# Closing pass of an adaLN block with attention and a mixture of experts: the residual add goes from GpSimd to VectorE, and half of the pair sums go from VectorE to TensorE

## The reference

```python
h = _layernorm(x, axis=-1) * (1 + ca) + sa
x = x + ga * _L0_attn_ref(h, ...)
h = _layernorm(x, axis=-1) * (1 + cb) + sb
x = x + gb * _L0_ffn_ref(h, ...)      # inside: return h + alpha * moe_out
```

## Time and profile before

| | us |
|---|---|
| three timed runs | 453.78, 459.27, 459.58 |
| their median | 459.27 |
| the profiled execution | 455.82 |
| its span (first to last instruction in the trace) | 454.0 |
| TensorE busy | 365.8 (81%) |
| VectorE busy | 312.9 (69%) |
| ScalarE busy | 268.6 (59%) |
| GpSimd busy | 258.4 (57%) |
| closing pass, from the first load's issue to the end of the span | 425.39 to 454.0 |

### The profile page before, as it was taken

One profiled execution on the slowest core, in us unless ns is written; L12 is line 12 of the kernel. 1 busy time (PEld: TensorE's weight loads), 2 busy tenths in 40 slices (PEclk: granted clock), 3 DMA queues, 4 the chain that ended last, 5 costly groups with the idle time before them and its releaser, 6 DMA issues.

```text
span 454.0 us, 11788 instructions
## 1 busy us (share of the span) xinstructions
PE 365.8 (81%) x3935; PEld 300.1 (66%) x3935; DVE 312.9 (69%) x948; ACT 268.6 (59%) x468; POOL 258.4 (57%) x306
## 2 busy tenths in 40 slices
PE   3728889988999999998779998939999999999100
PEld 1415667765766766665447997939999999998000
DVE  2506899999899999999967765624544444444194
ACT  2326789986888888886556668423555555554000
POOL 3010255878789898888763684654444444444264
PEclk9967999997999999999868999887999999999755
DMA  8355666656666666666865122231222122121494
GB/s 274 82 135 142 163 161 158 157 148 169 155 169 179 163 180 180 174 164 168 291 241 141 48 70 60 61 94 43 60 65 66 53 55 58 51 55 43 118 299 138
DMA packets 56027, 59.37 MB, mean 131 GB/s; under 512 B 7167, under 2 KB 48128, under 8 KB 55712
## 3 DMA queue, kind: packets, MB, share of 16 engines
q1 hardware_dynamic: 51648, 50.15, 42.4%
q0 software_dynamic: 4320, 8.47, 5.6%
HBM read 34.81 MB, written 24.23 MB: 130 GB/s over the span
## 4 chain that ended last, share of the span: by engine, by line
PE 35%; POOL 20%; SPq 14%; DMA 12%; issue 10%; DVE 5%; ACT 1%; POOLq 0%; ACTq 0%; DVEq 0%
PE SC L643 19%; POOL queue L1398 10%; PE OB L655 9%; DMA qdram<-rope 4%; POOL rstd L1390 3%; POOL gbh L1379 3%; SPq L352 3%; SPq L332 2%; SPq L362 2%; DVE pt L1313 2%; SPq L386 2%; DMA ydram<-ysb,xb 2%; PE FA L557 2%; SPq L347 2%; DMA stq<-qdram 2%
## 5 line engine op out<-in xcount | busy, mean ns | idle before, releaser
L1435 POOL DMA_INDIRECT ydram<-ysb,xb x71 | 69.4, 977 | 84.2 <-DVE ysb L1223 74.2
L643 PE MATMUL SC<-xTs,wgu 128*128 128x128 f32 x852 | 110.6, 281 | 4.6 <-issue 3.6
L643 PEld LDWEIGHTS SC<-xTs,wgu 128*128 128x128 f32 x852 | 103.1, 196 | 7.4 <-issue 5.8
L711 ACT ACTIVATE pt<-SC 128x1536 f32<-128x1536 f32 x64 | 92.6, 1447 | 25.9 <-PE SC L471 25.8
L944 DVE SCALAR_TENSOR_TENSOR pt<-pt,cst 128x1024 f32<-128x1024 f32 x64 | 81.2, 1268 | 13.6 <-ACT pt L711 13.5
L1398 POOL DMA_INDIRECT queue<-pl,dest x64 | 74.3, 1161 | 15.4 <-issue 14.8
L471 PE MATMUL SC<-stq,stk 24*128 24x256 f32 (+1 forms) x1024 | 64.1, 367 | 15.9 <-DMA stq<-qdram 12.0
L780 ACT ACTIVATE sg<-SC 128x384 f32<-128x384 f32 x71 | 34.8, 490 | 70.0 <-PE SC L643 69.4
L1157 DVE COPY xTs<-FA 128x128 f32<-128x128 f32 x71 | 20.7, 291 | 73.1 <-PE FA L557 64.6
L471 PEld LDWEIGHTS SC<-stq,stk 24*128 24x128 f32 x1024 | 49.3, 197 | 31.3 <-DMA stq<-qdram 13.5
L772 ACT ACTIVATE wgu<-gu,ws 128x704 f32 x71 | 62.1, 875 | 12.2 <-issue 12.1
(11 more groups left out here) (156 smaller groups left out, 524.4 us busy)
## 6 DMA issues: line engine op xcount, KB each, us to landing
stk<-kdram SPq DMA_DIRECT2D x64, 96.0 KB
stq<-qdram SPq DMA_DIRECT2D x64, 96.0 KB
xb<-queue SPq DMA_DIRECT2D x71, 65.0 KB, 1.8
kdram<-rope SPq DMA_DIRECT2D x32, 128.0 KB
qdram<-rope SPq DMA_DIRECT2D x32, 128.0 KB
bc<-modrow SPq DMA_DIRECT2D x16, 256.0 KB
pt<-ydram SPq DMA_DIRECT2D x16, 256.0 KB, 5.2
gu<-gup SPq DMA_DIRECT2D x1, 2816.0 KB
```

The costliest lines, as they stand in the source:

```text
L643: last = mm(GUB[b % 2][:, n, c * P:(c + 1) * P], wgu[:, b % 2, n, c * P:(c + 1) * P], xTs[:, b % DEEP, :], start=True, stop=True)
L711: af(pt[:, j, :, 0:S + P], SC[:, :, 0:S + P], ACT.Exp, scale=SCALE).then_inc(s["exp_done"], 1)
L1435: G.indirect_dma_start(ydram, bass.IndirectOffsetOnAxis(xb[:, slot(b), D + 1:D + 2].bitcast(u32), 0), ysb[:, slot(b), :], None, bounds_che ...
```

## The change

GpSimd's loop of 8 residual adds is gone, with its wait for `base_ready`. VectorE has the residual add now, as a third step of each chunk, and waits for `base_ready` once. The product with the gate is written to `ybuf[1]` and not in place. In chunks 1, 3, 5 and 7 VectorE no longer adds y0 and y1. TensorE does: it multiplies each with the identity matrix and lets the two products accumulate in a bank of PSUM, and VectorE's gate product reads that bank. Each of the four chunks has a bank of its own (FA, FB, BK, OB); the new semaphore `sum0` counts the finished banks.

```diff
+        SUMS = {1: FA, 3: FB, 5: BK, 7: OB}
 ...
+            need(pe, s["y_ready"], NBLK)
+            for n, bank in SUMS.items():
+                pe.wait_ge(s[f"yin{n}"], 2 * DMA)
+                for k in range(2):
+                    last = mm(bank[:, :], ident, ybuf[k][:, n * TCH * D:(n + 1) * TCH * D],
+                              start=(k == 0), stop=(k == 1))
+                last.then_inc(s["sum0"], 1)
 ...
             dve.wait_ge(s["gba_in"], DMA)
+            dve.wait_ge(s["base_ready"], B)
             bch = TCH // T
             for n in range(NCH):
-                dve.wait_ge(s[f"yin{n}"], 2 * DMA)
                 c0, c1 = n * TCH * D, (n + 1) * TCH * D
-                tt(ybuf[0][:, c0:c1], ybuf[0][:, c0:c1], ybuf[1][:, c0:c1], ALU.add).then_inc(s["sum1"], 1)
-                dve.wait_ge(s["sum1"], n + 1)
+                if n in SUMS:
+                    dve.wait_ge(s["sum0"], n // 2 + 1)
+                    both = SUMS[n][:, :]
+                else:
+                    dve.wait_ge(s[f"yin{n}"], 2 * DMA)
+                    tt(ybuf[0][:, c0:c1], ybuf[0][:, c0:c1], ybuf[1][:, c0:c1], ALU.add).then_inc(s["sum1"], 1)
+                    dve.wait_ge(s["sum1"], n // 2 + 1)
+                    both = ybuf[0][:, c0:c1]
                 for m in range(bch):
-                    y = ybuf[0][:, c0 + m * T * D:c0 + (m + 1) * T * D].rearrange("p (t d) -> p t d", d=D)
-                    last = tt(y, y, gba[:, n * bch + m:n * bch + m + 1, :].to_broadcast([P, T, D]), ALU.mult)
+                    part = slice(m * T * D, (m + 1) * T * D)
+                    last = tt(ybuf[1][:, c0:c1][:, part].rearrange("p (t d) -> p t d", d=D),
+                              both[:, part].rearrange("p (t d) -> p t d", d=D),
+                              gba[:, n * bch + m:n * bch + m + 1, :].to_broadcast([P, T, D]), ALU.mult)
                 last.then_inc(s["sum2"], 1)
+                dve.wait_ge(s["sum2"], n + 1)
+                tt(xall[:, c0:c1], xall[:, c0:c1], ybuf[1][:, c0:c1], ALU.add).then_inc(s["sum3"], 1)
 ...
-            pool.wait_ge(s["base_ready"], B)
-            for n in range(NCH):
-                pool.wait_ge(s["sum2"], n + 1)
-                c0, c1 = n * TCH * D, (n + 1) * TCH * D
-                G.tensor_tensor(xall[:, c0:c1], xall[:, c0:c1], ybuf[0][:, c0:c1], ALU.add).then_inc(s["sum3"], 1)
```

More of the change, by code:

```diff
@@ L271, in adaln_kernel @@
         GUB, XP, YP = (SC[:, 0:2, :], SC[:, 2:4, :]), FA, OB
+        SUMS = {1: FA, 3: FB, 5: BK, 7: OB}
         names2 = """table_step table_ready pad_ready padded z_wgu wgu_ready gba_in xt_done xts_ready gu_done
             sg_ready hid_ready y_done y_ready yin0 yin1 yin2 yin3 yin4 yin5 yin6 yin7
-            sum1 sum2 sum3 out_done""".split()
+            sum0 sum1 sum2 sum3 out_done""".split()
         s.update({n: sem(n) for n in names2})
```

## The result

| | before | changed |
|---|---|---|
| median of 17 runs each, us | 458.89 | 454.18 |
| lowest and highest | 453.78, 465.19 | 451.36, 457.39 |
| profiled execution | 455.82 | 453.18 |
| its span | 454.0 | 451.4 |
| issue of the first load | 425.39 | 426.43 |

The ratio of the times, changed over before, is 0.9928, with a 95% interval from 0.9901 to 0.9955. Of 458.89 us that is -3.3 us (-4.5 to -2.1). Times and profiles are compared between undisturbed executions; only the profile of e5 is of one that was 2.3% above the fastest of its kernel, and e6 was run just once.

The account below looks back on a forecast made before the run. VectorE, slowed by GpSimd, was taken to bound the closing pass, and GpSimd's drain the end. VectorE's 1.4 us and the drain's 2.4 made -3.8 us; from a 457.5 us median that gave 453.7, range 449.0 to 458.6.

Parts of the forecast that it names:

- VectorE slowed by GpSimd: Closing pass: without GpSimd's additions product pairs take 0.76 us, not 1.70; last residual add 1.4 us earlier.
- Products from PSUM cost the same: VectorE's gate products reading a PSUM bank: no difference taken from SBUF; some 65 ns more each by the skill.
- TensorE's first sum: Chunk 1 on TensorE at half clock: about 3.6 us, making VectorE wait 3.9 us once.
- The later sums: Chunks 3, 5, 7 on TensorE at half clock: ready at 438.9, 442.4, 446.0, no further wait of weight.
- The rival of a sum at 4.5 us: TensorE's weight loads stand between matmuls: 4.8 us a sum, time 458.5, deciding from 4.5 us; chance 0.03.
- The drain: GpSimd's closing drain at the program's end moves under the closing pass, over by 432; 2.4 us of SyncE's wait go.
- The sum: Whole kernel: span from 454.0 to 450.2 us, a change of -3.8 us; time named 453.7 us.

Follow-up runs that it names:

- e5: Changed kernel plus ten unread TensorE matmuls before the first sum, and the last chunk's residual add and store in two halves; ratio to before 0.9862.
- e6: Changed kernel, but TensorE forms each of its four sums twice into the same bank; one run, 454.29 us beside a before median of 457.59.
- e3: Changed kernel plus one GpSimd memset of 128x2 that waits for the last residual add and that nobody reads; ratio to before 1.0012.
- e1: Changed kernel without TensorE's sums: VectorE adds y0 and y1 in all chunks, GpSimd stays out of the pass; ratio to before 0.9928.
- e2: Changed kernel plus ten unread fp32 TensorE matmuls of 512 columns between the last block and the first sum; ratio to before 0.9862.
- e9: Second run of the changed kernel plus ten unread TensorE matmuls before the first sum; ratio to before 0.9868.

## Why the prediction was right, point by point

**VectorE slowed by GpSimd: right.** The products take 0.76 us a pair everywhere, and an even chunk 438.00 to 440.12 = 2.12 us (2.15 predicted). The last residual add came 1.4 us earlier in the pass, as forecast.

**Products from PSUM cost the same: right.** The rows by their source:

```profile
L1329 DVE TENSOR_TENSOR pt<-pt,stq x8: 418/422/425, 431.2 to 446.1; 128x256 f32<-128x256 f32 x8
L1329 DVE TENSOR_TENSOR pt<-FA,stq x2: 415/420/425, 436.6 to 436.9; 128x256 f32<-128x256 f32 x2
...
L1329 DVE TENSOR_TENSOR pt<-BK,stq x2: 414/415/416, 443.6 to 444.0; 128x256 f32<-128x256 f32 x2
```

415 to 420 ns from PSUM, 422 from SBUF. The 65 ns more that the Trainium skill ("VectorE: DVE Perf Modes", the TRN2 errata) would give for each are not there.

**TensorE's first sum: right to 0.1 us.** 3.75 us against 3.62, with the clock at 0.50. The rows of 256-column fp32 records were the ones to go by. The figure of the Trainium skill ("TensorE: Matmul & The Clock Gate", Back-to-back issue gap), 427 ns per 512 columns, would have made it 1.7; the trace has twice that time per column. The wait was 3.9 us, as worked out.

**The later sums: the size was off, without effect.** The prediction had TensorE at half clock for all four sums, almost level with VectorE (446.0 beside 446.06). The clock came back during the second:

```profile
436.00:438.00 2.00, 2.00 (x3) 0.84 (x3) 1.37 (x4) 0.00 (x0) 0.00 (x0) 0.50 1.17 290
438.00:440.00 2.00, 1.53 (x4) 0.47 (x3) 1.93 (x5) 0.00 (x0) 0.00 (x0) 0.86 1.20 291
440.00:442.00 2.00, 1.85 (x4) 0.54 (x4) 1.97 (x5) 0.00 (x0) 0.00 (x0) 1.00 1.20 293
```

From then on a sum takes 1.99 us and chunk 7 is ready at 445.24, 1.9 us before VectorE asks for it. The rival of a sum at 4.5 us needs much more than the weight loads: they stayed under the matmuls, at 0.33 us each, and e6 with 6 us for the first sum and 3.6 for the rest, 4.2 in the mean, is still ahead of before. No run has sums of 4.5 us, so the point itself stays an estimate.

**The drain: right.** It ran from 424.0 to 430.0, under the loads. That is 2.3 us of the gain, 2.4 predicted; e3 brings it back with one small memset.

**The sum.** Tail 450.2 - 425.4 = 24.8 predicted, 25.0 and 24.4 measured. The forecast was -3.8 us, the ratio says -3.3 (-4.5 to -2.1), the median 454.18 where 453.7 was named. That the named time came so close is partly luck. The four runs from which it started gave 457.5 as the time before, and all 17 gave 458.89; the medians then differ by 4.7 us, more than the forecast and more than the ratio says.

**What it did not ask.** The prediction priced the change as a whole, and its own numbers held the answer that e1 gave: four adds saved are 4 x 0.73 = 2.9 us, the wait brought in is 3.9. It wrote both down and did not set them against each other. A forecast of e1 from the same rows would have had it faster than the change.

## What to carry to other kernels

Read what ends the program behind the last work: here GpSimd, with a little work late, held the end with its closing drain, and moving that work elsewhere gained the drain as well. When work goes to an engine that has been idle, price its first piece at the low clock and ask what waits for it; here one wait of 3.9 us undid the four adds that were saved, and matmuls that nobody reads, run while the loads are under way, shortened the tail to 0.6 to 0.8 us less than with VectorE alone. GpSimd beside VectorE costs most where VectorE's operations read SBUF twice.

## What the runs showed of the hardware that was not expected

GpSimd's closing drain ends 4.8 us after its last work, whatever that was: additions of 1.3 us, an indirect DMA, a memset of 0.10 us. The drains of VectorE and TensorE end with their last work (in the changed kernel at 448.7 and 445.3). What the 4.8 us are spent on, no run here shows.

The granted clock after an idle stretch did not come back at the same point: during the second sum in the changed kernel's first profile, within the first in e3 (3.36 us) and in the second profile (3.52). The same ten matmuls took 8.85 (e2), 9.74 (e9) and 10.07 us (e5). In the last two the clock had fallen before they began. In e9 it was:

```profile
429.00:431.00 2.00, 1.42 (x6) 1.13 (x6) 0.28 (x2) 0.00 (x0) 1.21 (x2) 0.69 0.03 4
431.00:433.00 2.00, 1.64 (x2) 0.84 (x3) 0.30 (x1) 0.00 (x0) 0.92 (x1) 0.50 0.01 0
```

TensorE had been idle there for no more than 1.1 us at a stretch, in the gaps between the last matmuls of stage 2. In e2 the gaps were the same, and the clock stayed at 1.00.
